# Second layer of a two-layer network: the sums of the weighted scan states are formed on GpSimd instead of VectorE

## The reference, cut to what matters

```python
def _L0_attn_ref(x, Wz, bz, Wx, bx, WB, bB, WC, bC, Wdt, bdt, A_log, Wout, bout):
    ...
    def ssm_step(h, inp):
        a_t, x_t, c_t = inp
        h_new = a_t * h + x_t                      # scan along the 512 tokens, 128 x 16 states
        y_t = jnp.einsum('bdn,bn->bd', h_new, c_t) # weigh each of the 16 states by C, add them up
        return (h_new, y_t)
    ...
    y = y_ssm * z
    return y @ Wout + bout
...
x = x + s * g                                      # s: scan, g: silu of the mixture of experts
xn = _layernorm(x, axis=-1)
s = _L1_attn_ref(xn, ...)
g = _silu(_L1_ffn_ref(xn, ...))
x = x + s * g
```

## Time and profile before

| | |
|---|---|
| time, median of 3 runs | 1313.63 us (1307.95 to 1328.43) |
| profiled execution, span | 1322.4 us |
| PE busy | 1105.6 us, 84% |
| DVE busy | 976.9 us, 74% |
| ACT busy | 623.9 us, 47% |
| POOL busy | 297.1 us, 22% |
| mean granted TensorE clock | 0.922 |

### The profile page before, as it was taken

One profiled execution on the slowest core, in us unless ns is written; L12 is line 12 of the kernel. 1 busy time (PEld: TensorE's weight loads), 2 busy tenths in 40 slices (PEclk: granted clock), 3 DMA queues, 4 the chain that ended last, 5 costly groups with the idle time before them and its releaser, 6 DMA issues.

```text
span 1322.4 us, 19242 instructions
## 1 busy us (share of the span) xinstructions
PE 1105.6 (84%) x6765; PEld 689.4 (52%) x6765; DVE 976.9 (74%) x1514; ACT 623.9 (47%) x1111; POOL 297.1 (22%) x370
## 2 busy tenths in 40 slices
PE   7679999998767977888789888988988888898886
PEld 6567787787334434435444543543455354455353
DVE  6748878886488776986897698799889867654433
ACT  2647667663325424455346454553544543443421
POOL 2075555550313103202020320141032201000000
PEclk9779999999888878988899898998999989899898
DMA  7568777773363433253235325424533421310010
GB/s 201 162 217 250 234 221 232 231 223 100 98 127 98 113 81 95 78 118 102 64 96 120 108 77 102 119 78 111 114 112 87 102 48 34 57 42 19 17 50 8
DMA packets 91117, 150.24 MB, mean 114 GB/s; under 512 B 21032, under 2 KB 50032, under 8 KB 90960
## 3 DMA queue, kind: packets, MB, share of 16 engines
q1 hardware_dynamic: 67888, 72.33, 21.6%
q0 software_dynamic: 22976, 76.43, 19.3%
q10 hardware_dynamic: 160, 0.26, 0.2%
HBM read 124.33 MB, written 11.54 MB: 103 GB/s over the span
## 4 chain that ended last, share of the span: by engine, by line
PE 26%; DVE 22%; issue 9%; DMA 7%; ACT 7%; POOL 2%; another core or an unknown queue 2%; SPq 0%; DVEq 0%; POOLq 0%; ACTq 0%
PE bank L1235 5%; DVE neg_max L1709 4%; DMA rec_wide<-head_recips 3%; DVE sc_state L298 2%; ACT probs L1519 2%; PE bank L1264 2%; PE bank L1319 2%; PE bank L1381 2%; PE bank L1315 2%; PE bank L1283 2%; PE bank L1324 2%; PE bank L1241 2%; PE bank L1306 1%; ACT L1519 1%
## 5 line engine op out<-in xcount | busy, mean ns | idle before, releaser
L1519 ACT ACTIVATE probs<-bank 128x1024 f32<-128x1024 f32 (+1 forms) x192 | 169.1, 881 | 337.9 <-PE bank L1241 238.4
L1709 DVE TENSOR_REDUCE neg_max<-bank 128x2 f32<-128x1024 f32 (+3 forms) x256 | 204.2, 819 | 110.7 <-PE bank L1241 80.7
L1235 PE MATMUL bank<-q_all,kk 49*128 49x512 f32 (+3 forms) x1024 | 204.1, 498 | 49.2 <-ACT probs L1519 39.4
L212 POOL DMA_DIRECT2D sc_bc_wide<-scan_bc x128 | 73.1, 572 | 492.6 <-DVE sc_ub L291 254.7
L1235 PEld LDWEIGHTS bank<-q_all,kk 49*128 49x128 f32 x1024 | 88.1, 197 | 156.7 <-issue 66.5
L1283 PE MATMUL bank<-kr,q_all 48*128 48x512 f32 (+3 forms) x512 | 114.0, 481 | 51.3 <-DVE neg_max L1709 49.7
L779 PE MATMUL bank<-xcol,wst 128*128 128x256 f32 x624 | 149.7, 384 | 0.6 <-issue 0.6
L298 DVE TENSOR_TENSOR_SCAN sc_state<-sc_a,sc_ub 128x1024 f32<-128x1024 f32 x64 | 146.0, 2282 | 0.0
L900 POOL DMA_INDIRECT xrow<-sorted_in,token_of x78 | 103.1, 1322 | 120.5 <-PE bank L766 63.3
L779 PEld LDWEIGHTS bank<-xcol,wst 128*128 128x128 f32 x624 | 114.1, 193 | 13.6 <-issue 0.9
L1264 PE MATMUL bank<-probs,vaug 128*32 128x512 f32 (+3 forms) x1024 | 99.8, 487 | 0.0
(11 more groups left out here) (300 smaller groups left out, 1809.6 us busy)
## 6 DMA issues: line engine op xcount, KB each, us to landing
sc_bc_wide<-scan_bc POOLq DMA_DIRECT2D x128, 512.0 KB
wst<-in_wexp SPq DMA_DIRECT2D x39, 512.0 KB
q_all<-q_kind SPq DMA_DIRECT2D x94, 128.0 KB, 4.4
rec_wide<-head_recips SPq DMA_DIRECT2D x31, 256.0 KB
p_t<-gates_turned SPq DMA_DIRECT2D x14, 512.0 KB
sorted_out<-xrow SPq DMA_DIRECT2D x7, 640.0 KB
rows_all<-in_x SPq DMA_DIRECT2D x8, 256.0 KB, 4.4
sorted_in<-rows_all SPq DMA_DIRECT2D x8, 256.0 KB, 5.6
```

The costliest lines, as they stand in the source:

```text
L212: eng.dma_start(self.v["bc_wide"][:, n % 2, what, :, :], self.bc_d[b, first:first + PER, :].partition_broadcast(P)).then_inc(self.rows_in[ ...
L1235: mm(bank[1][:, par, at:at + n], kk[rows, b % 2, kt * P:(kt + 1) * P], q_all[rows, quad // 2 % 3, pair, kt * P:L].bitcast(F32), start=(at ...
L1519: af(probs[:, slot % RING, :, 0:width], bank[1][:, :, 0:width], ACT.Exp, scale=0.125).then_inc(s["p_ready"], 1)
L1709: last = v.tensor_reduce(neg_max[:, quad % 2, pr:4:2, i], bank[0][:, :, at:at + (i + 1) * P], AX, ALU.max, negate=True)
```

## The change

`add` takes the engine as an argument. In `experts0` VectorE goes on doing it (`on=v`). In `layer1` it is taken out of VectorE's program and put at the head of GpSimd's slot, ahead of `load_rows`, the gather and the roots. Its waits, its semaphores and its slot (S+3) are the same.

```diff
-    def add(self, dve, b, k):
+    def add(self, eng, b, k, on):
         s, v = self.s, self.v
-        dve.wait_ge(s["sc_hc"], b * NC + k + 1)
+        eng.wait_ge(s["sc_hc"], b * NC + k + 1)
         if k >= 2:
-            dve.wait_ge(s["sc_add"], (NC - 1) * b + k - 1)
-        self.nc.vector.tensor_tensor(v["y"][:], v["y"][:], v["ub"][:], ALU.add).then_inc(s["sc_add"], 1)
+            eng.wait_ge(s["sc_add"], (NC - 1) * b + k - 1)
+        on.tensor_tensor(v["y"][:], v["y"][:], v["ub"][:], ALU.add).then_inc(s["sc_add"], 1)
...
                     if (at := chunk_due(m - 3)) is not None and at[1] >= 1:
-                        scan.add(dve, *at)
+                        scan.add(dve, *at, on=v)
...
                 for slot in range(SLOT0, SLOT1):
+                    if (at := chunk_due(slot, 3)) is not None and at[1] >= 1:
+                        scan.add(pool, *at, on=g_)
                     if slot == SCAN_START - 7:
...
                         if at == (SCANNED, 0):
                             scan.enter(dve, SCANNED, 1)
-                    if (at := chunk_due(slot, 3)) is not None and at[1] >= 1:
-                        scan.add(dve, *at)
                     if (at := scan_due(slot, "gate")) is not None:
                         scan.gate(dve, at[0])
```

## The result

The changed kernel takes 1337.5 us (median of 4 runs, 1333.78 to 1342.15) against 1311.49 us before: ratio 1.0174, 95% interval 1.0125 to 1.0223. It is slower by 1.7%. That is under the 2% that were counted as no change, but the interval reaches beyond 2%, so the side of that line on which it lies is not settled. A second measurement, in a later group of runs, gave 1.0176 (1.0121 to 1.023). The ratios of the experiments leave out runs over 1.5% above the fastest of their kernel, which are 1 of 29, 4 of 26 and 4 of 29 runs of the kernel before in the three groups, and none of any other kernel. Means over all runs come out a little lower: 1.005 for e5 and e9, 1.002 for e7, 1.000 for e10.

What follows compares the result with a forecast made beforehand. PE and VectorE, both near full, were taken to wait for one another slot by slot. Relief -9.5, late adds +5 and port +5 gave +0.5 us on the 1313.63 median, rounded up to 1315 us; range 1300 to 1336.

Steps and rivals of the forecast that it cites:

- the neighbourhood of 1308 to 1322: Whole kernel: the forecast of 1315 us and the times around it, given a chance of 0.5.
- the second rival: GpSimd adds of 3.3 us and VectorE exclude each other; late `enter` and port cost 16 us each: 1334 us, chance 0.22.
- Length of an add: On GpSimd in layer 1: 2.2 us per add, from the slope of one-input copies, with 1.1 and 3.3 kept.
- Relief, -9.5 us: VectorE, layer 1: of 14.2 us of adds on the chain of waits, 9.5 us come back.
- Where the add is late: Behind the roots and first gather `enter` starts 9.1 us late together; somewhat over half counted, +5 us.
- The port, +5 us: Behind `weigh`, GpSimd's add stops VectorE instructions with two SBUF inputs (L1872, L1835, L1769): +5 us, ends 0 and 16.
- the later row DMAs: Row DMAs issued behind the add on GpSimd go out 2.2 us later; claimed to cost nothing.
- Signs: Changed profile: L315 on POOL at 2.0 to 2.5 us, VectorE's busy time down about 42 us, L1672 at 0.20.
- Relief winning outright: Rival: late adds absorbed, VectorE not waiting for GpSimd's port, adds off the chain counting: -14, 1300 us, chance 0.2.

Runs made afterwards that it cites:

- e5: Kernel before, plus 35 pairs of GpSimd fills that read nothing, at the places the change gives the adds; ratio 1.0083.
- e9: Kernel before, plus 30 pairs of GpSimd fills that read nothing, none between the roots and roots2; ratio 1.0062.
- e7: Changed kernel with only the adds of slots 9, 13 and 17 of each 24 (18) on GpSimd, the others on VectorE; ratio 1.0047.
- e10: Changed kernel, late adds back on VectorE, 29 on GpSimd, four kinds waiting for VectorE's two-SBUF-input instruction behind `weigh`; ratio 1.0009.
- e1: Kernel before, the 35 adds staying on VectorE but cut to the first 2 of 512 columns; ratio 0.9953.
- e2: Changed kernel, each of the 35 GpSimd adds cut to the first 2 of 512 columns; ratio 0.9925.
- e12: Changed kernel with only the six late adds (behind roots and first gather) on GpSimd, the other 29 on VectorE; ratio 1.0075.
- e6: Changed kernel with the six late adds (behind roots and first gather) back on VectorE, 29 left on GpSimd; ratio 1.006.
- e3: Kernel before, plus 35 spare two-input adds on GpSimd at the change's places, which nobody reads or waits for; ratio 1.0071.

## Why the prediction was right, and short in its size

The forecast was no change that can be told, 0.1% slower at 1315 us, and the measured one is 1.7% slower, within 2% and at the upper end of the range of 1300 to 1336: 1.0174 times the 1313.63 us it was made against is 1336.5, and times the 1311.49 us of the four runs 1334.3. The late add and the mutual stops were named and were found, but the neighbourhood of 1308 to 1322 that had half of the chances was missed by over 12 us, and it was the width of the range that held the result. The time is the one that the second rival gave (1334), though not by its price: the adds are 2.35 us long, not 3.3, and its terms as written add up to +22.5, not +20.

- **Length of an add: right.** 2.2 us estimated from the slope of the copies, 2.35 measured.
- **Relief, -9.5 us: right within what was measured.** e1 and e2 give -6 and -10, each with 4 us either way. Counting the adds on the chain, and half of those with PE close behind, gave a fair size, perhaps a little too much.
- **Where the add is late: right in place and wait, wrong in worth.** The two places were the roots and the first gather. At the roots `enter` came 1.2 us late (1.1 worked out). At the first gather it waited 4.00 us and started at 419.02 instead of 414.75, partly since the gather itself ran later. The term that was too small is "I count somewhat over half of it on the path, +5 us". The six adds alone cost 0.75% (e12), 10 us, and putting them back took 1.2% off the changed kernel. Both figures hold the stops of L1815 too, which the working did not have. That the idle time ahead of the next reduction is no slack, since PE waits in turn, would explain it, but no run shows that, and behind the first gather the delay did shrink.
- **The port, +5 us: perhaps the right size, wrong list.** e6 against e10, the same adds with and without VectorE being stopped, is 0.5%, 6 to 7 us, but with half a per cent either way and on two chips; e3 against the fills shows no difference at all. So between nothing and 1% fits. L1769 stood for 7.7 us over five times (three times 1 us was worked out, and 1 us counted), L1835 for 1.8 us in three of six. L1872 was never stopped, since GpSimd waited for it instead; by the prediction's own numbers it would have been delayed by 1.4 us (2.2 less 0.8), not 1.5 to 1.9. L1886 (+4.0 us) and L1815, which has one SBUF tensor as input, were not in the sum.
- **What no step had:** some 0.5 to 0.8% for a long instruction on GpSimd as such (e5, e9, and the rest in e10). With 0.6% for it the terms are -0.75% relief, +0.75 to 1.2% late adds, +0.5% port, +0.6% this: +1.1 to 1.55%, against 1.74% measured with an interval of half a per cent either way. The terms overlap, since the late adds bring stops and relief of their own, so this is a comparison of sizes and not a proof. Where the last term comes from stays open. The one way to it that the prediction had, the later row DMAs, it put at nothing; no run tried them alone.
- **Signs.** L315 on POOL came at 2.34 to 2.37 us in 27 of 35, and L1672 at 0.20, as forecast. VectorE's busy time was to fall by about 42 us and fell by 24, and L1872 was to be longer and was not. `enter` waited in no ordinary chunk.
- **Chances.** Relief winning outright (0.2) is refuted by the result, and e1 and e2 show why: even with no cost at all the kernel would be 0.5 to 0.75% faster, not 1%.

## What to carry to other kernels

Before an instruction is moved from VectorE to GpSimd, measure the most that it can bring, by shrinking it where it stands: here 43 us of busy time were worth 6 to 10. Then look at what the GpSimd queue holds when the operands are ready, and at what VectorE runs in the 2.35 us behind: here the add held nothing up where GpSimd was idle and VectorE ran no instruction with two SBUF inputs behind it. A wait put in front of the add, until VectorE's two-input instruction is through, removed the mutual stops entirely and made `enter` wait nowhere. Even so the kernel was only as fast as before, so here the add is best left on VectorE.

## What the runs showed of the hardware

- A float32 add of 128 x 1024 with both inputs in SBUF takes 2.35 us on GpSimd and 1.215 us on VectorE.
- GpSimd's add and VectorE's instructions with two SBUF inputs exclude each other for a whole instruction, in both directions (2.71 us for 0.69; 4.72 us for 2.35). By the Trainium skill (SBUF — State Buffer, Who interferes with whom) that is so; the trace agrees, now in the direction too that the kernel before could not show. The recorded starts do not tell which of the two gets in (the add recorded 0.29 us ahead of L1872 is the one that stood).
- GpSimd fills of 1.18 us, which read nothing, stopped no VectorE instruction with two SBUF inputs. At one place they stopped a tensor_scalar with one (796 and 862 ns, against 286 at most).
- VectorE's tensor_scalar on float32 in SBUF, with its scalars from SBUF, was stopped by the add too. DVE and POOL of the changed kernel at 1000 us (four pieces that take 1.12 us together in the kernel before):

```profile
1000.11 3.16 DVE L1815 TENSOR_SCALAR xn<-xt,mv,rstd 128x128 f32<-128x128 f32 x4
...
1000.48 2.45 POOL L315 TENSOR_TENSOR sc_y<-sc_y,sc_ub 128x1024 f32<-128x1024 f32 x1
```
